# A perceiver block on Trainium2: the probabilities-times-values products of a tile step, in one stretch at its end

## What is computed

```python
scale = D ** (-0.5)
qh = (q @ Wq.T).reshape(B, Lq, H, D).transpose(0, 2, 1, 3)
kh = (k @ Wk.T).reshape(B, Lk, H, D).transpose(0, 2, 1, 3)
vh = (v @ Wv.T).reshape(B, Lk, H, D).transpose(0, 2, 1, 3)
qh = _layernorm(qh, gq, bq) * scale
kh = _layernorm(kh, gk, bk)
attn = jax.nn.sigmoid(jnp.einsum('bhqd,bhkd->bhqk', qh, kh))
x = jnp.einsum('bhqk,bhkd->bhqd', attn, vh)
```

## Time and profile before

| | |
|---|---|
| median of three runs | 3382.52 us |
| profiled execution, span | 3380.9 us |
| TensorE busy | 3248.4 us, 96% |
| VectorE busy | 2106.5 us, 62% |
| ScalarE busy | 2060.2 us, 61% |
| GpSimd busy | 1136.4 us, 34% |
| first step of the attention loop starts | 57.7 us |
| its last score products start | 2289.1 us |

### The profile page before, as it was taken

One profiled execution on the slowest core, in us unless ns is written; L12 is line 12 of the kernel. 1 busy time (PEld: TensorE's weight loads), 2 busy tenths in 40 slices (PEclk: granted clock), 3 DMA queues, 4 the chain that ended last, 5 costly groups with the idle time before them and its releaser, 6 DMA issues.

```text
span 3380.9 us, 69200 instructions
## 1 busy us (share of the span) xinstructions
PE 3248.4 (96%) x23066; PEld 2489.2 (74%) x23066; DVE 2106.5 (62%) x3531; ACT 2060.2 (61%) x3237; POOL 1136.4 (34%) x859
## 2 busy tenths in 40 slices
PE   6999999999999999999999999997899999999998
PEld 4666666666666666666666666663799898999897
DVE  6565565656565565656556565655557767557867
ACT  2777777777777777777777777771244544445444
POOL 3333334333333334333333434330103223112222
PEclk8999999999999999999999999997899999999999
DMA  4000000000000000000000000000254454544443
GB/s 181 25 22 25 22 23 24 22 25 22 25 22 25 22 22 25 22 25 22 25 22 24 23 22 25 22 7 25 106 181 162 162 186 162 188 163 176 161 174 131
DMA packets 53230, 231.78 MB, mean 69 GB/s; under 512 B 6040, under 2 KB 6296, under 8 KB 31776
## 3 DMA queue, kind: packets, MB, share of 16 engines
q1 hardware_dynamic: 53152, 230.73, 20.2%
HBM read 230.19 MB, written 0.52 MB: 68 GB/s over the span
## 4 chain that ended last, share of the span: by engine, by line
PE 89%; DVE 5%; issue 3%; ACT 1%; DMA 1%; POOL 1%; ACTq 0%; DVEq 0%; POOLq 0%; SPq 0%
PE kv_ps L1061 37%; PE f_ps L1319 17%; PE o_ps L1105 13%; PE s_ps L1096 12%; PE t_ps L1087 4%; PE y_ps L1306 3%; DVE stage L926 1%; ACT w_hi L555 1%; DVE h_hi L925 1%; PE pm L1188 1%; DMA w_raw<-w_dram 1%; DVE sums L1019 1%; DVE w_lo L648 0%; POOL h_lo L472 0%; PE pm L1177 0%
## 5 line engine op out<-in xcount | busy, mean ns | idle before, releaser
L498 ACT ACTIVATE probs<-s_ps 128x1024 f32<-128x1024 f32 x784 | 803.3, 1025 | 594.4 <-PE s_ps L1096 594.3
L697 DVE CAST kT<-t_ps 64x256 fp32r<-64x256 f32 x784 | 326.6, 417 | 650.9 <-PE t_ps L1087 639.2
L419 POOL TENSOR_TENSOR k_var<-k_var,neg_half 128x16 f32<-128x16 f32 x196 | 570.7, 2911 | 15.4 <-POOL k_var L415 0.2
L409 POOL TENSOR_TENSOR ctx_lo<-ctx_raw,ctx_hi 128x512 fp32r<-128x512 f32 x196 | 251.8, 1285 | 951.2 <-DVE ctx_hi L689 951.2
L1096 PEld LDWEIGHTS s_ps<-q,kT 128*128 128x128 f32 x3136 | 421.9, 189 | 167.8 <-issue 159.6
L648 DVE TENSOR_TENSOR w_lo<-w_raw,w_hi 128x2048 fp32r<-128x2048 f32 x164 | 381.9, 2333 | 254.3 <-ACT w_hi L555 254.1
L1096 PE MATMUL s_ps<-q,kT 128*128 128x256 f32 x3136 | 526.5, 290 | 7.2 <-ACT kT L507 4.9
L1105 PE MATMUL o_ps<-probs,v_sb 128*32 128x256 f32 x6272 | 503.6, 393 | 0.1
L472 POOL TENSOR_TENSOR h_lo<-stage,h_hi 128x256 f32 x240 | 253.0, 1068 | 725.7 <-DVE h_hi L928 410.9
L1319 PE MATMUL f_ps<-h_hi,w_hi 128*128 128x256 f32 x1536 | 429.4, 280 | 9.6 <-POOL h_lo L472 9.6
L1319 PE MATMUL f_ps<-h_lo,w_hi 128*128 128x256 f32 x1536 | 428.0, 279 | 0.0
(11 more groups left out here) (202 smaller groups left out, 5419.7 us busy)
## 6 DMA issues: line engine op xcount, KB each, us to landing
w_raw<-w_dram SPq DMA_DIRECT2D x160, 1024.0 KB, 4.8
ctx_raw<-ctx_dram SPq DMA_DIRECT2D x196, 256.0 KB, 2.7
qkv_w<-qkv_w_dram SPq DMA_DIRECT2D x1, 3072.0 KB, 12.7
bias_rows<-bias_rows_dram SPq DMA_DIRECT2D x1, 1280.0 KB, 16.8
wq<-wq_dram SPq DMA_DIRECT2D x1, 1024.0 KB, 5.6
wk_rows<-wk_dram SPq DMA_DIRECT2D x1, 1024.0 KB, 7.6
wv<-wv_dram SPq DMA_DIRECT2D x1, 1024.0 KB, 9.7
out_w<-out_w_dram SPq DMA_DIRECT2D x1, 1024.0 KB, 17.8
```

The costliest lines, as they stand in the source:

```text
L419: g.tensor_tensor(k_var[:, 2], k_var[:, 1], neg_half[:].to_broadcast([P, H]), ALU.pow)\
L498: s.activation(probs[grp][:], s_ps[:], ACT.Sigmoid).then_inc(probs_made, 1)
L697: v.tensor_copy(kT[grp][0:P // 2, :, 0], pairs[0:P // 2]).then_inc(kt_even_made, 1)
```

## The change

The four calls of `attend` leave the quarters and follow all four quarters of the step, in the same order of groups: first groups 2 and 3 of tile r - 2, then groups 0 and 1 of tile r - 1. The group number goes from q - 3 to q - 2, so that the group whose scores are made in the last quarter is attended in the same step. One call behind the last step goes, as the step now contains it. Nothing else changes, neither on TensorE nor on another engine.

```diff
@@ step, in the loop over the four quarters
                         projection(it, r, half_way, a1)
                     if not too_early(it, r, q - 1):
                         turn_keys(it, *group(r, q - 1))
-                    if not too_early(it, r, q - 3):
-                        attend(it, *group(r, q - 3))
+                for q in range(4):
+                    if not too_early(it, r, q - 2):
+                        attend(it, *group(r, q - 2))
@@ behind the last step
             step(nq, 4, project_it=False)
             turn_keys(nq, 3, 3)
             scores(nq, 3, 2)
-            attend(nq, 3, 1)
             scores(nq, 3, 3)
             attend(nq, 3, 2)
             attend(nq, 3, 3)
```

## The result

The changed kernel is slower: 3628.51 us (median of four runs, 3624.97 to 3629.1) against 3383.26 us before, a ratio of 1.0714 (95% interval 1.0699 to 1.0729). The profiled execution has a span of 3627.1 us, 246.2 more than before. The forecast was 3581 us. The result lies inside the stated range, 3540 to 3650, but above 3610, where the forecast's own share of that range ended.

The account below looks back on a forecast made before the run. TensorE's own instruction stream was taken to bound the kernel. New step 8.13 + 4.26 = 12.39 us against 11.363, 1.03 more; 194 steps give +199 us, 3581 us to the median, range 3540 to 3650.

Parts of the forecast that it names:

- the forecast's own share of that range: Whole kernel: 3540 to 3610 us, from shorter waves and shorter or longer loops; forecast given 78%.
- The loop as the new bound: Three quarters without attend: scores, sigmoid, kT copies, next scores take 2.61 us, above TensorE's 2.13, so scores wait.
- 2.61, 2.68 and 2.84 us for the three quarters: Scores to scores in the quarters without attend, set by ScalarE's loop; together 8.13 us.
- these 0.30 us slack: Kernel before: ScalarE's second kT copy ends 0.30 us ahead of the scores, called all the slack the quarter has.
- So today the loop is set by TensorE's own instruction stream, and by nothing else: Attention loop before the change: TensorE busy in every microsecond of 500 us; scores waited only 7.2 us in all.
- The quarter with the stretch, 4.26 us: Quarter 3 on TensorE: scores to turn_keys, turn_keys, block of attends 1.94 us, four projections; sum 4.26 us.
- The saving of 0.76 us a step: TensorE's attends in one stretch: one entry and exit a step instead of four, work 2.84 to 2.08 us.
- rival B: Stretch of attends: they don't follow without a break, block 2.28 us, +0.34 a step, 3647 us; chance 12%.
- A: Attention loop: next scores don't wait for ScalarE's loop, saved entries and exits come through, 3235 us; chance 6%.
- C: TensorE's clock in the loop: new waits lower it, at half clock about 5280 us; chance 3%.
- D: Whole step: waits and saving cancel, no difference, with a loop of some 2.2 us in three quarters; chance 1%.
- The signs to look for: Changed profile: scores waiting for L507 0.4 to 0.7 us in three quarters, step 12.4 us, one long ScalarE idle piece.

Follow-up runs that it names:

- e6: Changed kernel with turn_keys and both engines' copies into kT one quarter earlier, the stretch of attends left at the step's end: 3288.7 us, ratio 0.9726.
- e3: Kernel before, with ScalarE's two copies into kT cut to 8 of 128 columns: 3354.4 us, ratio 0.9907.
- e8: Kernel before, with the wait for probs_made put ahead of the two waits for kT in scores: 3359.3 us, ratio 0.9928.
- e10: Changed kernel with turn_keys a quarter earlier, attend stretch ending quarter 1, square before group 1's copies, keys split before VectorE's last two copies: 3191.7 us, ratio 0.9432.
- e11: Kernel before (attends in their quarters) with turn_keys and kT copies a quarter earlier, keys split before VectorE's last two copies: 3355.4 us, ratio 0.9922.
- e1: Changed kernel with the wait for probs_made put ahead of the two waits for kT in scores: 3590.8 us, ratio 1.0598.

## Why the prediction was right, and where its size was off

**The loop as the new bound: right, shown by removal.** Shortening ScalarE's copies (e2) takes away 227 of the 245 us, and giving both engines' copies a quarter's lead (e6) takes away all of it, with the stretch left in place.

**2.61, 2.68 and 2.84 us for the three quarters: mis-sized.** Measured 2.75, 2.83 and 2.84. The step that failed is the reading of the loop's length from the earlier trace rows. The rows were right, and the steps behind the loop of the changed kernel repeat them to 0.01 us. But within the loop the release takes 0.24 us from the copy's end, not 0.10. The first two quarters are 0.14 and 0.15 longer. In the third the scores at its start came later, yet the sigmoid was held by square and not by them, so 0.13 us were given back (0.78 us from scores to sigmoid, not 0.91) and 0.14 added at its end. The number could have been had: in the earlier trace rows ScalarE's second copy ended at 1003.43, and e3 and e8 show that the scores of 1003.73 had lost 0.03 us to it. I called these 0.30 us slack, part of it latency. There was no slack: 0.23 us passed until the scores' first weight load at 1003.66, and its lead over the matmul was 0.07 us, where it is 0.23 when nothing waits (2250.59 to 2250.82).

**"So today the loop is set by TensorE's own instruction stream, and by nothing else": wrong by some 25 us.** Seven to nine thousandths were being lost to ScalarE's loop, with no idle time of the matmuls to show it. e8 and e3 get them back (ratios 0.9928 and 0.9907), and the page of the profile had them as idle time of the scores' weight loads, which the prediction doesn't look at.

**The quarter with the stretch, 4.26 us: 4.21 measured.** The block took 1.87 us where 1.94 was forecast, 7 waves at 0.22 and not 0.23. **The saving of 0.76 us a step: real, and 0.84.** TensorE's busy step is 10.39 us in e10 against 11.36 before. Of the 0.97 between them 0.12 are the four times 0.03 that the kernel before lost; 0.84 are the stretch, by e10 and e11.

**The sum and the range.** 12.63 - 12.39 = 0.24 us a step, 47 us, which is what lies between forecast and result. The forecast's own range ended at 3610 us, with 0.05 us for each loop where two of them were off by 0.14 and 0.15. The stated range reached the result only because it had been carried on to 3650 for rival B, which did not happen: the mechanism was right, and that the range held was luck.

**The rivals.** A did not happen in the changed kernel, and its condition was the right one: in e6 and e10, where the loop is below TensorE's quarter, the kernel comes out at 3289 and 3192 us, beside A's 3235. By the rule of the Trainium skill's "Key Properties" ("TensorEngine Tiling (Array Packing)"), that a change of mode drains TensorE, fewer changes gain, and e10 against e11 agrees: 0.28 us for each entry and exit saved. How much of this is the drain and how much the first projection's weight load, the runs don't tell apart. B did not happen: 32 matmuls ran as eight waves without a break. C did not happen in the loop, where the granted clock stayed at 1.00 with three waits of 0.5 us a step. D did not happen; its loop was worked out wrongly too. By the prediction's own terms no difference needs loops of (11.363 - 4.26) / 3 = 2.37 us, not 2.2.

**The signs to look for** appeared but for one: L1096 waiting for L507 in three quarters of four, 0.48 or 0.49 us each and 291 us in all (about 300 forecast), a row of 32 matmuls of 1.93 us, TensorE at 88% (some 85% forecast). The one that failed is ScalarE's idle time in one long piece a step: there is a long piece of 2.27 us before the first sigmoid, but pieces of 1.0 us stay before two of the other three, the time from a copy through the next scores to their sigmoid.

## What to carry to other kernels

An engine at 100% with a small gap to the next loop is balanced, not free. The idle time of its weight loads can show that where its matmuls show none (168 us here, 91 with the loss gone). So before work is gathered from several places into one, measure the loop that this work was covering, scores to scores through the other engine. Gather it only after that loop has been taken off the path (here by issuing turn_keys one quarter earlier and splitting the keys first), and the saving of entries and exits then comes through, 5.7% here. And read a latency where the code stands in the same form: steps behind a loop had constants in their waits, steps inside it had not.

## What the runs showed of the hardware

- Inside the loop, scores with three waits of their own started 0.24 us after the end of ScalarE's copy when it ended the second wait (changed kernel), and 0.14 us after it when it ended the third (e1). Behind the loop, with constants, the same were 0.09 and 0.14 us. So a satisfied wait behind an unsatisfied one cost 0.10 us, and only with a value from the loop's register.
- A release 0.30 us before the matmul cost 0.03 us a quarter that no view shows as idle time of the matmuls; the scores took 0.51 us and not 0.48 until the next projection started. The weight loads showed it: 0.20 us idle before the first one (kernel before, 1003.66).
- Going from full-array products to 32-column ones and back cost 0.28 us each time, the late weight load of the first full-array product included (e10 against e11).
- With 32-column products of 256 fp32 columns, four side by side, a wave took 0.22 us, over four groups with their own waits between.
